# A pair-of-heads loop with registers, written out eight times with constants

## The reference

```python
q, k, v = shape(h @ wq), shape(h @ wk), shape(h @ wv)      # h = layernorm(x)
scores = jnp.einsum('bhqd,bhkd->bhqk', q, k) + compute_bias(rel_bias, s, s)
attn = jax.nn.softmax(scores, axis=-1)
x = x + layernorm(einsum('bhqk,bhkd->bhqd', attn, v) @ wo)
```

## Time and profile before

| | |
|---|---|
| median of 3 runs | 3138.8 us (3134.37 to 3140.66) |
| profiled execution | 3133.59 us, span 3131.6 us |
| PE busy | 2860.9 us (91%) |
| POOL busy | 2277.1 us (73%) |
| DVE busy | 1894.2 us (60%) |
| ACT busy | 1647.3 us (53%) |
| mean granted TensorE clock | 0.979 |
| instructions | 56771 |

### The profile page before, as it was taken

The page is one execution under the profiler, slowest core; times in us unless marked ns, Lnnn a source line. Parts: engine busy times, 40 slices in busy tenths (PEclk is TensorE's granted clock), DMA queues, the critical chain, the costliest instruction groups (busy, mean ns, idle before and its releaser), DMA issues.

```text
span 3131.6 us, 56771 instructions
## 1 busy us (share of the span) xinstructions
PE 2860.9 (91%) x18785; PEld 1056.0 (34%) x18785; DVE 1894.2 (60%) x4727; ACT 1647.3 (53%) x2139; POOL 2277.1 (73%) x1033
## 2 busy tenths in 40 slices
PE   3499999999999999999999989999999999997887
PEld 1133333333333333333333333333333333322343
DVE  5565656566566656566556556565656656576676
ACT  2255555554555555554555545555555555556566
POOL 0088878888788878887888878887888888887100
PEclk9699999999999999999999999999999999999999
DMA  7000000000000000000000000000000000100001
GB/s 159 17 1 2 2 2 19 1 2 2 19 1 2 1 2 19 1 2 2 19 2 2 1 19 1 2 2 1 19 1 2 2 8 1 55 1 1 28 1 54
DMA packets 45691, 37.36 MB, mean 12 GB/s; under 512 B 21510, under 2 KB 43782, under 8 KB 45366
## 3 DMA queue, kind: packets, MB, share of 16 engines
q1 hardware_dynamic: 45366, 33.34, 4.1%
HBM read 28.39 MB, written 11.34 MB: 13 GB/s over the span
## 4 chain that ended last, share of the span: by engine, by line
PE 57%; issue 17%; DVE 15%; ACT 7%; DMA 1%; SPq 1%; DVEq 0%; ACTq 0%; POOL 0%; POOLq 0%
PE po L609 20%; PE st L579 17%; PE pre L591 6%; PE pm L547 4%; ACT prob L888 4%; DVE mpart L1238 3%; PE st L809 3%; DVE st L1255 3%; PE pm L639 3%; PE pm L553 2%; DVE pre L1235 2%; PE pm L618 1%; ACT o L921 1%; DMA t_scratch<-w_scratch 1%; ACT qk L869 1%
## 5 line engine op out<-in xcount | busy, mean ns | idle before, releaser
L519 POOL TENSOR_TENSOR acc<-acc,prob 128x1024 f32<-128x1024 f32 x896 | 2116.8, 2362 | 470.7 <-ACT prob L888 429.8
L888 ACT ACTIVATE prob<-st 128x1024 f32<-128x1024 f32 x1024 | 1016.0, 1021 | 1014.2 <-DVE st L1255 733.0
L609 PE MATMUL po<-prob,v 128*64 128x512 f32 x4096 | 994.9, 606 | 0.0
L579 PE MATMUL st<-qk 64*128 64x512 f16 x6144 | 843.4, 381 | 20.3 <-ACT prob L888 17.3
L1230 DVE CUSTOM_DVE_ANT_0 pre<-pre,ew 128x512 f32<-128x512 f32 x448 | 300.8, 713 | 587.1 <-issue 587.1
L1235 DVE CUSTOM_DVE_ANT_0 pre<-pre,tab 128x512 f32<-128x512 f32 x704 | 475.8, 716 | 107.8 <-issue 106.7
L579 PEld LDWEIGHTS st<-qk 64*128 64x128 f16 x6144 | 295.0, 95 | 350.7 <-ACT prob L888 58.4
L591 PE MATMUL pre<-qk 64*128 64x512 f16 x1600 | 312.7, 387 | 94.1 <-DVE mpart L1238 35.3
L609 PEld LDWEIGHTS po<-prob,v 128*64 128x64 f32 x4096 | 248.9, 136 | 439.2 <-issue 369.6
L579 PE MATMUL st<-eq,ek 64*128 64x512 f16 x2048 | 392.9, 380 | 0.0
L1238 DVE TENSOR_REDUCE mpart<-pre 128x2 f32<-128x1024 f32 x224 | 274.0, 1223 | 115.9 <-PE pre L591 112.9
(11 more groups left out here) (186 smaller groups left out, 2367.9 us busy)
## 6 DMA issues: line engine op xcount, KB each, us to landing
t_scratch<-w_scratch SPq DMA_DIRECT2D x2, 3072.0 KB
inv_r<-inv SPq DMA_DIRECT2D x260, 1.0 KB, 1.7
y<-x SPq DMA_DIRECT2D x2, 2048.0 KB, 11.6
qk<-x SPq DMA_DIRECT2D x8, 512.0 KB, 5.8
out<-qk SPq DMA_DIRECT2D x8, 512.0 KB, 3.8
w<-w_pairs SPq DMA_DIRECT2D x8, 384.0 KB, 3.8
t2f<-t_scratch SPq DMA_DIRECT2D x8, 384.0 KB, 4.6
t<-t_scratch SPq DMA_DIRECT2D x8, 384.0 KB, 3.2
```

Source lines behind the costliest of these rows:

```text
L519: nc.gpsimd.tensor_tensor(acc[g % 2][:, :, :], a, prob[:, n % RING, :, :], ALU.add).then_inc(sum_p, 1)
L579: last = nc.tensor.matmul(st[:, 2 * (n % 2) + h, :], w[64 * h:64 * h + 64, :], t[64 * h:64 * h + 64, :], start=(r == 0), stop=(r == len(te ...
L609: last = nc.tensor.matmul(po[64 * h:64 * h + 64, :], v[:, g // CHUNKS, j, 64 * h:64 * h + 64], prob[:, n % RING, h, :], start=(s == 0), st ...
L888: nc.scalar.activation(prob[:, n % RING, :, :], st[:, 2 * (n % 2):2 * (n % 2) + 2, :], ACT.Exp).then_inc(exp_done, 1)
```

## The change

In five places the loop on the engine is replaced by a Python loop of the same bounds, so that the body is emitted once per pair and i is a number. The order of the instructions on each engine, the tiles, the semaphores and their counts stay the same. The code of pair 7 is not touched, but for GpSimd's, which was in its loop.

```diff
-            with sp.Fori(0, PAIRS - 1) as i:
+            for i in range(PAIRS - 1):
                 tables_in(i, False)
...
-            with pool.Fori(0, PAIRS) as i:
+            for i in range(PAIRS):
                 for n in range(STEPS):
...
-            with pe.Fori(0, PAIRS - 1) as i:
+            for i in range(PAIRS - 1):
                 pair_of_heads(i, False)
             pair_of_heads(PAIRS - 1, True)
...
-            with act.Fori(0, PAIRS - 1) as i:
+            for i in range(PAIRS - 1):
                 pair_of_heads(i, False)
...
-            with dve.Fori(0, PAIRS - 1) as i:
+            for i in range(PAIRS - 1):
                 pair_of_heads(i, False)
```

## The result

| | before | after |
|---|---|---|
| median | 3139.4 us of 4 runs (3134.37 to 3140.66) | 3097.91 us of 4 runs (3097.29 to 3098.99) |
| profiled execution | 3133.59 us, span 3131.6 us | 3097.29 us, span 3095.5 us |
| instructions in the trace | 56771 | 49866 |

The ratio is 0.987, 95% interval 0.985 to 0.989: 41.5 us faster by the medians, where 40.6 us were forecast. The two profiled executions differ by only 36.3 us.

What follows compares the result with a forecast made beforehand. PE was taken to pace each round, with edge stalls and register arithmetic on the chain of waits; 13.4 + 25.2 + 2 = 40.6 us gained, median 3098 us, range 3082 to 3116 us (8 in 10).

Steps and rivals of the forecast that it cites:

- Term 1: Edges between loop rounds, seen in slot 0: six backward branches at 2.2 us in the mean, 13.4 us gained.
- code loading moves: Rival at the former edges: straight code waits there for its next block too, 3111 to 3116 us; chance 0.12.
- Term 2: Register arithmetic before waits, mainly ACT's exponential: about 0.15 us per band step on the chain, 25.2 us over seven pairs.
- the ruler: Spacing of the copies ending each slot, used to compare equal work with and without edges or registers.
- Term 3: GpSimd's loop and the bias table in slot 6: constants gain 0.3 us for each of seven tables, 2 us.
- the clock only as something to gain: Slot 6 rival, table's stall dissolves: PE's clock falls behind stalls would go too, some 10 us; about 3067 us; chance 0.07.
- The sum: Whole kernel: 40.6 us gained, span 3091.0 us, median 3098 us after carrying over 5.2 us from profiled execution to median.
- The check list: Signs: no COMPARE_BRANCH, slot 0 41.3 to 41.5 us, pairs 338.5 to 339 us apart, about as many instruction blocks.
- straight code fetched late: Rival within the rounds: instruction blocks come late by 2.2 us each, about 3150 us and up; chance 0.05.

Runs made afterwards that it cites:

- experiment 2: Kernel before with constants and no loop on one engine alone: ScalarE 3117.77 us, TensorE 3137.47 us, VectorE 3137.42 us.
- experiments 2 and 3: The second: see experiment 2. The third: changed kernel with one engine keeping its loop and registers: ScalarE 3134.42 us, TensorE 3109.36 us.
- experiment 5: Changed kernel with VectorE's instruction count to be shifted ahead of pair 0: 64 empty instructions (left no trace) 3096.83 us, 32 one-element memsets 3096.63 us.

## Why the prediction was right

**Term 1, the edges: right.** 13.4 us were forecast. Slot 0 with registers and no edge takes 41.9 us on the mean against 44.1 us, 6 x 2.2 = 13.2 us; by the medians the step is 15.7 us (the reason may be the clock, see the sum below). Pair 2, with 1.9 us by its slot 0 of 43.8 us, did not lie between 2.0 and 2.9 us as I wrote; the mean of 2.2 us was right. The rival "code loading moves" is out: slot 0 has 41.3 us in every pair. The remark that the stalls run side by side was right, but incomplete: I took ScalarE's as the one on the chain, and TensorE's alone costs nearly the same.

**Term 2, the arithmetic: right in size and place.** Forecast 25.2 us; measured 24.6 us between registers kept and constants, 20.9 us of it with ScalarE alone. Slots 1, 2, 4, 5 and 7 gained 0.4 us each, as the ruler had said; slot 3 gained 0.6 us. It has the split of weights, left out of my comparison and with registers of its own; that these make the difference was not tested. The mechanism was the forecast one, 0.15 us at each such step (experiment 2).

**Term 3, the table: not gained in the mean.** I had 0.5 us from term 2 and 0.3 us from term 3 for each slot 6, 5.6 us over seven. TensorE's wait did shorten by 0.2 us, but slot 6 went from 48.6 to 48.7 us. What I missed stands in my own: the clock's fall behind the stall. In the profiled execution before, slot 6 took 48.5 to 48.7 us in every pair. In the changed kernel it takes 48.0 to 49.3 us. The granted clock in windows behind the stalls of pairs 4 and 5:

```profile
1795.00:1802.00 7.00, 5.48 (x26) 2.07 (x26) 3.04 (x10) 2.98 (x4) 3.37 (x2) 0.51 0.00 1
...
2136.00:2140.00 4.00, 3.61 (x18) 1.30 (x20) 0.92 (x3) 2.98 (x4) 1.94 (x1) 0.57 0.00 0
```

In pair 4 the lower level (1.2 GHz) holds for nearly all of 7 us, in pair 5 for less than 4 us, although both stalls are alike; slot 6 takes 49.3 and 48.3 us there. The short fall is the one that all seven slots 6 had before. Where it stayed short (pairs 0, 1, 3 and 5), slot 6 takes 48.0 to 48.3 us and did gain, 0.4 us in the mean; the long falls of pairs 2, 4 and 6 took 1 us each and with it the gain. I had spoken of the clock only as something to gain.

**The sum: right by an offset.** Against its own execution the sum was 4.5 us too good: span 3091.0 us forecast, 3095.5 us measured, about what slot 6 kept back. The median came out at 3097.9 us against 3098 us since the profiled execution before was a short one: of 13 runs of that kernel measured later the shortest had 3133.14 us at a granted clock of 0.979, the longest 3143.08 us at 0.971. The profiled one had 3133.59 us at 0.979. Adding 5.2 us for its distance to the median was a scaling without a cause, and that the two errors cancelled was luck. The changed kernel keeps to 3095.8 to 3099.0 us over its runs and those of its twin with one-round loops, so it gained on the executions of before that are longer.

Part of a cause can be seen in the traces of experiments 2 and 3. In the five kernels there that keep a loop somewhere, the granted clock fell behind 7 of 30 edges, and slot 0 then took 45.1 to 46.5 us, elsewhere 42.2 to 44.8 us. The profiled execution before has no such fall, and no straight kernel has one. With 2 us for each, an estimate from these slots, an execution with all edges loses 7/30 x 6 x 2 = 2.8 us more than the ruler's 13.2 us, which comes near the medians' 15.7 us. That this and slot 6 make the 5 us is argued, not shown: over the 42 runs of the kernel before that were made beside the experiments, time and clock go together only loosely (those at 0.978 or 0.979 took 3133.1 to 3136.8 us, those at 0.973 3135.3 to 3143.5 us), and no run holds the clock fixed.

**The check list.** No backward branch, the slot lengths, and the longest L1202 of 2.5 us came as written. There is no sequencer instruction between addition and exponential. The step from pair to pair is 339.5 us, above the 338.5 to 339 us, again slot 6. The count of instruction blocks fell by 84, which I had not expected. The mechanism that would have made the kernel slower, straight code fetched late, exists in miniature (experiment 5): four pauses of 0.35 us on the path, 1.4 us.

## What to carry to other kernels

A loop on the engines has two prices that can be read from one trace: the step over its edge against the same work without one, and the work in front of each wait against a copy of the body that has constants; look for such a copy, as the last round here. The second was the larger one, it sat on a single engine, in front of the one instruction whose release was late, and most of it could have been had by writing out that engine alone. And what a stall keeps is not only its length: two engines that shut each other out cost 2.1 us at one instruction, and the stall behind it lowered TensorE's clock, so moving the work away from the collision was worth 29.2 us, more than two thirds of the whole change.

## What the runs showed of the hardware

- One engine's backward branch is enough for nearly the full price of an edge: 2.1 us in the mean with TensorE's loop alone (0.9 us where its branch takes 3.6 us, 2.1 us where it takes 4.7 us), 2.3 us with ScalarE's alone, 2.2 us with all. TensorE loads 168 blocks of instructions with its loop and 148 without.
- VectorE's copy and tensor_scalar between places in SBUF wait out GpSimd's running sum (1470 instead of 559 ns, 2496 instead of 405 ns), while its row maxima over PSUM (L1238) take between 1195 and 1227 ns at all 224 places, beside a sum or not.
- In straight code VectorE pauses for 0.35 us at some of the passages from one block of 128 instructions to the next; four of these lengthened a slot.
- A semaphore count computed in a register costs where the wait behind it is late: two sequencer instructions moved 308 exponentials from 0.034 to 0.185 us behind the addition that released them.
- After like stalls of 4.1 us TensorE's granted clock stayed at the lower level for 3.4 or for 6.8 us, a difference of 1 us in slot 6. After stalls of 2.0 us it fell behind four of seven (0.9 to 1.4 us each), after stalls of 1.3 us behind none.
